# Four of the seven products of a pair accumulated in one PSUM bank, with ScalarE copies between

## What is computed

```python
x = x + attention(layernorm(x), Wq, bq, Wk, bk, Wv, bv, Wbeta, bbeta, Walpha, balpha)
xt = layernorm(x).reshape(2048, 512)
Wg, Wu = dequant(gate codes, gate scales), dequant(up codes, up scales)    # 4096 x 512
Wd = dequant(down codes, down scales)                                      # 512 x 4096
gate, up = xt @ Wg.T, xt @ Wu.T
inter = gelu_tanh(gate) * up
x = x + (inter @ Wd.T).reshape(4, 512, 512)
```

## Time and profile before

| | us |
|---|---|
| median of 3 runs | 1166.65 (1166.26 to 1167.24) |
| the profiled execution | 1165.97 |
| its span in the profile | 1164.2 |
| TensorE busy | 1150.1 (99%) |
| VectorE busy | 834.7 (72%) |
| POOL busy | 505.4 (43%) |
| ScalarE busy | 395.9 (34%) |

### The profile page before, as it was taken

One profiled execution on the slowest core, in us unless ns is written; L12 is line 12 of the kernel. 1 busy time (PEld: TensorE's weight loads), 2 busy tenths in 40 slices (PEclk: granted clock), 3 DMA queues, 4 the chain that ended last, 5 costly groups with the idle time before them and its releaser, 6 DMA issues.

```text
span 1164.2 us, 19595 instructions
## 1 busy us (share of the span) xinstructions
PE 1150.1 (99%) x7793; PEld 761.9 (65%) x7793; DVE 834.7 (72%) x1383; ACT 395.9 (34%) x835; POOL 505.4 (43%) x503
## 2 busy tenths in 40 slices
PE   8799999999999999999999999999999999999998
PEld 5556655566544445777777777777777777777775
DVE  7978554555666765987788778777877787777554
ACT  4343432435133232333333333333323333332221
POOL 2476332334155764335633563446344634462110
PEclk9999999999999999999999999999999999999999
DMA  8021010000020010110011001100110010100011
GB/s 299 20 66 45 28 37 10 19 19 19 1 73 1 19 37 19 37 37 20 19 37 37 19 19 37 38 19 19 37 37 26 22 41 23 37 19 11 37 37 64
DMA packets 22683, 41.94 MB, mean 36 GB/s; under 512 B 2688, under 2 KB 2752, under 8 KB 22592
## 3 DMA queue, kind: packets, MB, share of 16 engines
q1 hardware_dynamic: 22592, 40.70, 11.0%
HBM read 36.46 MB, written 4.23 MB: 35 GB/s over the span
## 4 chain that ended last, share of the span: by engine, by line
PE 96%; DVE 2%; POOL 1%; issue 0%; ACT 0%; DMA 0%; DVEq 0%; POOLq 0%; ACTq 0%
PE ps L459 38%; PE ps L486 28%; PE ps L422 14%; PE ps L327 9%; PE ps L381 1%; PE ps L295 1%; PE ps L364 1%; PE ps L388 1%; PE ps L375 1%; PE ps L355 1%; DVE wf L1010 0%; PE ps L305 0%; DVE XT L824 0%; DMA X<-x 0%; DVE bigA L818 0%
## 5 line engine op out<-in xcount | busy, mean ns | idle before, releaser
L486 PE MATMUL ps<-WR,ihl_s 128*128 128x512 f16 x768 | 175.7, 379 | 0.0
L422 PE MATMUL ps<-XT,WR 128*128 128x512 f16 x768 | 170.4, 379 | 0.0
L486 PE MATMUL ps<-WR,vv 128*128 128x512 f16 x720 | 164.7, 379 | 0.0
L459 PE MATMUL ps<-XT,WR 128*128 128x256 f16 x1152 | 157.1, 273 | 0.0
L459 PE MATMUL ps<-REG,WR 128*128 128x256 f16 x1152 | 157.1, 273 | 0.0
L975 DVE SCALAR_TENSOR_TENSOR X<-ps,X 128x512 f32<-128x512 f32 x128 | 88.1, 688 | 75.2 <-PE ps L486 74.5
L459 PEld LDWEIGHTS ps<-XT,WR 128*128 128x128 f16 x1152 | 112.7, 98 | 33.5
L422 PEld LDWEIGHTS ps<-XT,WR 128*128 128x128 f16 x768 | 75.0, 98 | 90.3 <-DVE fw L955 0.9
L486 PEld LDWEIGHTS ps<-WR,ihl_s 128*128 128x128 f16 x768 | 75.2, 98 | 79.7
L459 PEld LDWEIGHTS ps<-REG,WR 128*128 128x128 f16 x1152 | 112.7, 98 | 13.0
L486 PEld LDWEIGHTS ps<-WR,vv 128*128 128x128 f16 x720 | 70.4, 98 | 74.8 <-DVE vv L961 0.2
(11 more groups left out here) (174 smaller groups left out, 1901.6 us busy)
## 6 DMA issues: line engine op xcount, KB each, us to landing
load<-codes SPq DMA_DIRECT2D x48, 256.0 KB
load<-scales SPq DMA_DIRECT2D x48, 256.0 KB
y<-X SPq DMA_DIRECT2D x16, 256.0 KB, 2.0
bigA<-cla SPq DMA_DIRECT2D x14, 256.0 KB, 3.2
X<-x SPq DMA_DIRECT2D x3, 1024.0 KB, 12.8
WR<-wqkv SPq DMA_DIRECT2D x2, 1024.0 KB, 9.5
X<-x SPq DMA_DIRECT2D x4, 256.0 KB, 4.4
WR<-wqkv SPq DMA_DIRECT2D x4, 256.0 KB, 4.9
```

What stands on the lines that cost most here:

```text
L422: mm = eng.matmul(bank[:, :], buf[:, wp, o + kt, 128 * j:128 * j + 128], XT[:, xp, kt, 512 * b:512 * b + 512], start=(n == 0), stop=(n == 11))
L459: mm = eng.matmul(half_bank(kind, name), w(wp, kt), x(xp, kt), start=(n == 0), stop=(n == 5))
L486: mm = eng.matmul(PS[bank][:, :], ih[:, ip, 128 * tt:128 * tt + 128], buf[:, wp, 8 + j, :], start=(m == 0), stop=(m == 11))
```

## The change

- PSUM: P1, P6, P7 and P4 of a kind go to one bank (`chain`), P1 with start, the others adding on. P5 and P3 go to a second (`side`), P3 adding on to P5. P2 has a third (`last`).
- ScalarE copies the chain bank after P1 (start of C11), after P6 (of C12) and after P7 (of C22) to SBUF; C21 is the bank itself after P4. VectorE makes three additions: C11 + P2, C22 + P5, C12 + (P5 + P3).
- TensorE's order in a set is P1, P5, P2, P6, half a down, P7, the other half, P4, P3, with a wait for each copy before the next product of the chain, and for C22 before P3.
- gelu and inter of the odd tile are done in two halves of 256 (from C22 and from the bank).
- `dq_bits` stands behind the addition C11 of gate. The difference of `dq_chain` is moved ahead of the two `inter_low` on POOL (`dq_difference`), and ScalarE's four casts of `dq_sums` are spread between the copies of up.
- The four downs of group 31 run over banks 6, 7, 2, 3, first the halves (0, 1) of all, then the halves (3, 2).

```diff
-PRODUCT = {name: n + 1 for n, name in enumerate(("P1", "P5", "P7", "P6", "P4", "P3", "P2"))}
-COMBINED = {name: n + 1 for n, name in enumerate(("U2", "U3", "odd", "ends", "even"))}
+PRODUCT = {name: n + 1 for n, name in enumerate(("P1", "P5", "P2", "P6", "P7", "P4", "P3"))}
+COMBINED = {name: n + 1 for n, name in enumerate(("C11", "C22", "C12"))}
+PIECES = {name: n + 1 for n, name in enumerate(("C22", "C21", "even"))}
...
+            chain, side, last = (2, 3, 4) if kind == "gate" else (0, 1, 5)
+            bank = {"P1": chain, "P6": chain, "P7": chain, "P4": chain, "P5": side, "P3": side, "P2": last}[name]
+            return PS[bank][:, 0:256]
...
+                elif kind == "gate":
+                    pe.wait_ge(s_gelu, piece(m - 1, "C21"))
                 else:
-                    pe.wait_ge(s_comb, pair_base(kind, m - 1, 5) + COMBINED["even"])
+                    pe.wait_ge(s_inter, piece(m - 1, "C21"))
...
-                    n = 0
+                    first, n = name in ("P1", "P5", "P2"), 0
...
+                            mm = eng.matmul(half_bank(kind, name), w(wp, kt), x(xp, kt),
+                                            start=(first and n == 0), stop=(n == 5),
+                                            skip_group_check=True)
...
                 product("P1", left(0, e0), toks(0, 0))
+                if m > 16:
+                    pe.wait_ge(s_comb, pair_base(kind, m - 1, 3) + COMBINED["C12"])
                 product("P5", left(0, o0), sums(0))
-                if kind == "up":
-                    pe.wait_ge(s_comb, pair_base("gate", m, 5) + COMBINED["U3"])
-                elif m > 16:
-                    pe.wait_ge(s_comb, pair_base("up", m - 1, 5) + COMBINED["U3"])
+                product("P2", left(2, e0), toks(2, 0))
+                pe.wait_ge(s_snap, pair_base(kind, m, 3) + 1)
+                product("P6", comb(0), sums(1))
+                down(n, tt, (0, 1))
+                pe.wait_ge(s_snap, pair_base(kind, m, 3) + 2)
                 product("P7", comb(1), sums(2))
-                product("P6", comb(0), sums(1))
-                pe.wait_ge(s_snap, pair_base(kind, m, 2) + 2)
+                down(n, tt, (3, 2))
+                pe.wait_ge(s_snap, pair_base(kind, m, 3) + 3)
                 product("P4", left(2, o0), sums(3))
+                pe.wait_ge(s_comb, pair_base(kind, m, 3) + COMBINED["C22"])
                 product("P3", comb(2), toks(2, 256))
-                product("P2", left(2, e0), toks(2, 0))
...
+            def down(n, tt, js=(0, 1, 2, 3)):
+
...
+                if js[0] == 0:
+                    bank_of["dn", n, tt] = banks.take(pe, (s_ev, 4 * n + tt + 1))
+                bank, end = bank_of["dn", n, tt], js[-1] if js[-1] != 1 else None
+                for j in js:
...
+                                        start=(j == 0 and p == 0), stop=(j == end and p == 2))
+                if end is not None:
+                    mm.then_inc(s_dn, 1)
...
+                products("up", m, n, 2 * m % 4 + 1)
+            banks.ring = [6, 7, 2, 3]
+            banks.turn = 0
+            pe.wait_ge(s_gelu, piece(NI // 2 - 1, "C21"))
+            pe.wait_ge(s_comb, pair_base("gate", NI // 2 - 1, 3) + COMBINED["C12"])
+            for tt in range(4):
+                down(NI // 4 - 1, tt, (0, 1))
+            for tt in range(4):
+                down(NI // 4 - 1, tt, (3, 2))
...
+                parts = [(flat4(tS), high(1)), (a21, tiles(WR[g % 2][:, 0, base:base + 2, :], 1)), (a11, high(0)),
+                         (a12, high(2))]
+                for j in range(first, last):
+                    ac.wait_ge(s_chain, 4 * (pair_count(k) - 1) + j + 1)
+                    eng.copy(parts[j][1], parts[j][0]).then_inc(s_shi, 1)
...
+            def snapshot(kind, m, name):
+
+                v = vals[kind]
+                start = {"P1": v[:, 0, 0:256], "P6": v[:, 0, 256:512], "P7": v[:, 1, 256:512]}[name]
...
+                done, k = pair_base("gate", m, 3), 6 * (m // 8 + 1) + (1 if m % 8 == 4 else 3)
+                paired = m % 8 in (4, 7)
+                snapshot("gate", m, "P1")
                 if m > 16:
                     inter_high(oo - 2)
                     inter_high(ee - 2)
-                ac.wait_ge(s_comb, pair_base("gate", m, 5) + COMBINED["ends"])
-                gelu(oo, vals["gate"][:, 1, :])
-                ac.wait_ge(s_comb, pair_base("gate", m, 5) + COMBINED["even"])
+                snapshot("gate", m, "P6")
+                snapshot("gate", m, "P7")
+                ac.wait_ge(s_comb, done + COMBINED["C22"])
+                gelu(oo, vals["gate"][:, 1, 256:512], 256)
+                ac.wait_ge(s_prod, pair_base("gate", m, 7) + PRODUCT["P4"])
+                gelu(oo, half_bank("gate", "P4"))
+                if paired and m < 56:
+                    dq_sums(k, 0, 2)
+                snapshot("up", m, "P1")
+                ac.wait_ge(s_comb, done + COMBINED["C12"])
                 gelu(ee, vals["gate"][:, 0, :])
-                snapshots("up", m)
-                if m % 8 in (4, 7):
-                    if m < 56:
-                        dq_sums(6 * (m // 8 + 1) + (1 if m % 8 == 4 else 3))
-                elif dk < 48:
+                if paired and m < 56:
+                    dq_sums(k, 2, 3)
+                snapshot("up", m, "P6")
+                if paired and m < 56:
+                    dq_sums(k, 3, 4)
+                snapshot("up", m, "P7")
+                if not paired and dk < 48:
...
+            def inter(i, pu, done, at=0):
+                w = fw[:, i % 2, at:at + pu.shape[1]]
+                dv.wait_ge(s_gelu, done)
+                eng.scalar_tensor_tensor(w, w, GS * IS, pu, ALU.mult, ALU.mult).then_inc(s_inter, 1)
...
-            def combine(kind, m):
-                v, at = vals[kind], pair_base(kind, m, 5)
-                e1, u2, o1, u3 = v[:, 0, 0:256], v[:, 0, 256:512], v[:, 1, 0:256], v[:, 1, 256:512]
-                snap, prod = pair_base(kind, m, 2), pair_base(kind, m, 7)
-                dv.wait_ge(s_snap, snap + 1)
-                dv.wait_ge(s_prod, prod + PRODUCT["P6"])
-                eng.tensor_tensor(u2, e1, half_bank(kind, "P6"), ALU.add).then_inc(s_comb, 1)
-                dv.wait_ge(s_comb, at + 1)
-                dv.wait_ge(s_prod, prod + PRODUCT["P7"])
-                eng.tensor_tensor(u3, u2, half_bank(kind, "P7"), ALU.add).then_inc(s_comb, 1)
-                dv.wait_ge(s_comb, at + 2)
-                dv.wait_ge(s_prod, prod + PRODUCT["P4"])
-                eng.tensor_tensor(o1, u3, half_bank(kind, "P4"), ALU.add).then_inc(s_comb, 1)
-                dv.wait_ge(s_comb, at + 3)
-                dv.wait_ge(s_snap, snap + 2)
-                eng.tensor_tensor(v[:, :, 256:512], v[:, :, 256:512], s5b.unsqueeze(1).broadcast_to([128, 2, 256]),
-                                  ALU.add).then_inc(s_comb, 1)
-                dv.wait_ge(s_comb, at + 4)
-                dv.wait_ge(s_prod, prod + PRODUCT["P2"])
-                eng.tensor_tensor(v[:, 0, :], v[:, 0, :], PS[2 if kind == "gate" else 0][:, :],
-                                  ALU.add).then_inc(s_comb, 1)
+            def combine(kind, m, name):
+
+                v, end = vals[kind], {"C11": "P2", "C22": "P5", "C12": "P3"}[name]
+                c = {"C11": v[:, 0, 0:256], "C12": v[:, 0, 256:512], "C22": v[:, 1, 256:512]}[name]
+                dv.wait_ge(s_snap, pair_base(kind, m, 3) + {"C11": 1, "C12": 2, "C22": 3}[name])
+                dv.wait_ge(s_prod, pair_base(kind, m, 7) + PRODUCT[end])
+                eng.tensor_tensor(c, c, half_bank(kind, end), ALU.add).then_inc(s_comb, 1)
...
+                done = pair_base("up", m, 3)
+                combine("gate", m, "C11")
                 if (m == 16 or m % 8 not in (0, 5)) and dk < 48:
                     dq_bits(dk)
-                combine("gate", m)
+                combine("gate", m, "C22")
+                combine("gate", m, "C12")
                 gather(n, 2 * m % 4)
+                combine("up", m, "C11")
                 if m % 8 not in (4, 7) and dk < 48:
                     dq_finish(dk)
                     dk += 1
-                combine("up", m)
-                dv.wait_ge(s_comb, pair_base("up", m, 5) + COMBINED["ends"])
-                inter(oo, vals["up"][:, 1, :])
-                dv.wait_ge(s_comb, pair_base("up", m, 5) + COMBINED["even"])
-                inter(ee, vals["up"][:, 0, :])
+                combine("up", m, "C22")
+                dv.wait_ge(s_comb, done + COMBINED["C22"])
+                inter(oo, vals["up"][:, 1, 256:512], piece(m, "C22"), 256)
+                dv.wait_ge(s_prod, pair_base("up", m, 7) + PRODUCT["P4"])
+                inter(oo, half_bank("up", "P4"), piece(m, "C21"))
+                combine("up", m, "C12")
+                dv.wait_ge(s_comb, done + COMBINED["C12"])
+                inter(ee, vals["up"][:, 0, :], piece(m, "even"))
...
+            def dq_difference(k):
+                if k == 13:
```

(69 more changed lines are left out.)

61 lines of the change are left out of this document (5 added, 56 removed).

## The result

The changed kernel takes 1180.8 us in the median (1180.6 to 1182.35, 4 runs), the kernel before 1166.45 in its 4 runs beside it: a ratio of 1.0129 (95% interval 1.0117 to 1.0142), 14.4 us slower. The forecast was 1183.6 (range 1175 to 1195). The profiled execution's span grew from 1164.2 to 1178.9.

The account below looks back on a forecast made before the run. TensorE was taken as the bound, without a gap through the pairs. Stalls of 15 and 1.9 us onto the profiled 1165.97 gave 1182.9, and 0.68 to the median 1183.6 us; own range 1181.6 to 1192.6, whole range 1175 to 1195.

Parts of the forecast that it names:

- Copies of ScalarE hold up nothing: In each set, ScalarE's copies before P6, P7 and P4 finish 0.7 to 0.9 us early, at cost 0.
- Alternation: VectorE and POOL take turns: a VectorE operation ends 0.59 us (narrow 0.28) after the POOL operation met, POOL's next 1.01 later.
- the second branch: In pairs with a chain on POOL, the first bit operation gets in before POOL and it all ends 0.2 us earlier.
- The moment at which P3 is due: P3 of gate, which waits for C22, was due 6.52 us into the pair.
- The zero of t: Start of a pair's time scale, the first matmul of P1 of gate, put at 747.74 in the timeline shown.
- plain pairs: The 22 pairs running dq_bits without a chain on POOL: C22 ends at 6.15, margin 0.37 us, cost 0.
- the sign: TensorE idle before P3 of gate, ten times, 1.3 to 2.4 us each; never before P3 of up.
- the ten pairs: Pairs with dq_bits and a chain on POOL: TensorE stands 1.5 us before P3 of gate, 15 us in all.
- Rival 1: POOL pauses while dq_bits runs in the ten pairs, so only the end costs: 1168.6 us, not slower; chance 0.11.
- Rival 3: VectorE at half speed beside POOL: the four bit operations need about 4.3 us, stall 0.7 x 10: 1175.6 us; chance 0.06.
- The end: Behind the last P3, the second half of the group 31 downs waits for a bank's gather: stall 1.9 us, bounds 0 and 3.2.
- the two terms: The stall in the ten pairs, 15 us, and the stall behind the last P3, 1.9 us: 16.9 us together.

Follow-up runs that it names:

- the fifth operation: Changed kernel with one more narrow VectorE operation on spare SBUF behind the first bit operation in the ten pairs: 1202.88 us.

## Why the prediction was right

- *TensorE is the bound, VectorE's relief is worth 0.* Right: 121 us less of VectorE and no gain. It is 2.5 us per pair, where up to 4 was named. With the stalls away the pairs take 674.52 us against 674.42.
- *Copies of ScalarE hold up nothing.* Right; TensorE never waited for one.
- *Alternation.* 0.59 and 0.28 us behind the POOL operation met gave ends at 4.55, 5.84 and 7.56; measured 4.38, 5.68, 7.35. That comes to the second branch that the prediction named (all 0.2 earlier): the difference ended at t = 2.52 where 2.67 was worked out, and the first bit operation, begun 0.12 us before that, took its short time. The 0.59 is 0.04 too long: the earlier trace rows and all the traces give 0.54 to 0.55. Stall 1.40 for 1.5, 14.0 us for 15.
- *The moment at which P3 is due.* The zero of t, 747.74, was taken 0.17 us too late: by TensorE's rows P1's first matmul starts at 747.57, 0.91 before its copy. With zero there and P3 at 6.52 behind it, P3 is due at t = 6.35 of the prediction's scale, as pair 35 has it. So its own ends would have given a stall of 1.65, and the margin in plain pairs was 0.2, not 0.37. That the stall came out within 0.1 is in part luck: this error and the ends that came 0.2 earlier point opposite ways. For the same reason the idle times in the rows, 0.81 and 1.22, aren't the 1.3 to 2.4 that the prediction named as the sign; the 1.40 by distances is, at its low end. One of the four bit operations also kept its short time in the ten pairs, where four at 1.3 to 1.6 us were named.
- *Plain pairs.* C22 at 6.10 for 6.15; no stall in any of the 22, though the margin was the smaller one just named. Rival 1 falls with pair 36: POOL had no hole and three of the four operations waited. Rival 3 too: a milder contention would have left the four at 4.3 us (measured 4.95), and the fifth operation cost 1.27 where shares would have given 0.3 to 0.6.
- *The end.* Idle 1.92 for 1.9; 2.09 by the cut.
- *What was left out.* The sum took everything around the two terms as unchanged. Behind the last gather 1.1 us went and 0.4 in the start; with 1.0 less stall and 0.2 more at the end that is 2.3 of the 2.8 us between 1183.6 and 1180.8. The other 0.5 is the step from the profiled execution to the median, 0.68 in the sum and 0.2 in the changed kernel. The largest single error is the stretch behind the end: I held the last write to be as far from the last gather as before, and in nine of nine profiles with the change it is 3.1 us in place of 4.3. Because of these terms the median lies 0.8 us below the forecast's own range (1181.6 to 1192.6), though both stalls lie within their bounds; only the whole range, down to rival 3, holds it.

## What to carry to other kernels

Where one engine has no gap, count only what can make it wait, and put each new wait against the queue of the engine that is to release it. A VectorE operation like the bit operations here, with all its operands in SBUF, costs a whole turn of POOL when POOL's queue is full: count the turns ahead of the awaited instruction, not the microseconds of work, and move such operations to a stretch where POOL has less to do. A second wait can lie inside the first and comes out when the first is mended.
